# Last stage of a post-norm attention and mixture-of-experts layer: rows multiplied in ahead into eight PSUM banks, gate diagonals made during the experts, scaling on ScalarE, one load a batch

## What is computed

```
x = layernorm(x + attention(x))            # 16 heads of 8, causal
w = the two largest of softmax(x @ gate.T) # 14 experts, renormalised to sum 1
moe = w0 * expert[i0](x) + w1 * expert[i1](x)   # 128 -> 256, gelu, 256 -> 128
out = layernorm(x + clip(x + moe, -100, 100))
```

## Time and profile before

| | |
|---|---|
| median of 3 runs | 584.14 us (582.62 to 586.64) |
| the profiled execution's own time | 584.61 us |
| its span in the profile | 582.8 us |
| TensorE, VectorE, ScalarE, GpSimd busy | 454.8, 395.4, 319.7, 281.5 us |
| mean granted TensorE clock | 0.916 of full |
| experts, first to last TensorE work | 403.3 to 535.6 us |
| last stage, first load to last store issued | 540.6 to 577.8 us |

### The profile page before, as it was taken

The page is one execution under the profiler, slowest core; times in us unless marked ns, Lnnn a source line. Parts: engine busy times, 40 slices in busy tenths (PEclk is TensorE's granted clock), DMA queues, the critical chain, the costliest instruction groups (busy, mean ns, idle before and its releaser), DMA issues.

```text
span 582.8 us, 12473 instructions
## 1 busy us (share of the span) xinstructions
PE 454.8 (78%) x3544; PEld 279.2 (48%) x3576; DVE 395.4 (68%) x974; ACT 319.7 (55%) x771; POOL 281.5 (48%) x443
## 2 busy tenths in 40 slices
PE   4488999999999889999999997302877777766690
PEld 1244444444454444454454452102876666666690
DVE  4387679989889779889989984630454444444195
ACT  3065666776766756776767658102545454444570
POOL 2012233346556436556456448563565665556084
PEclk9599999999999989999999999755889898889697
DMA  7855942342542532442532301034322322210652
GB/s 130 254 164 168 299 147 87 112 152 86 156 147 75 156 120 81 151 148 74 156 120 89 90 30 43 10 98 95 96 79 69 83 76 69 69 58 20 180 164 91
DMA packets 82505, 65.46 MB, mean 112 GB/s; under 512 B 9207, under 2 KB 77950, under 8 KB 82449
## 3 DMA queue, kind: packets, MB, share of 16 engines
q1 hardware_dynamic: 75632, 55.52, 33.9%
q0 software_dynamic: 4512, 8.54, 4.4%
q10 hardware_dynamic: 2304, 0.74, 0.6%
HBM read 37.41 MB, written 25.85 MB: 109 GB/s over the span
## 4 chain that ended last, share of the span: by engine, by line
PE 58%; DVE 13%; issue 9%; ACT 5%; DMA 5%; POOL 3%; SPq 2%; another core or an unknown queue 2%; ACTq 0%; DVEq 0%; POOLq 0%
PE psum L873 10%; PE psum L855 9%; PE psum L832 8%; PE psum L1038 7%; PE psum L1027 7%; DVE nmax L1115 6%; PE psum L840 3%; PE psum L1017 3%; PE psum L892 3%; PE psum L928 2%; ACT probs L693 2%; PE psum L899 2%; POOL xs_dram L645 2%; DVE ov L1121 1%
## 5 line engine op out<-in xcount | busy, mean ns | idle before, releaser
L693 ACT ACTIVATE probs<-psum 128x512 f32<-128x512 f32 x320 | 182.3, 595 | 105.3 <-PE psum L855 73.5
L1115 DVE TENSOR_REDUCE nmax<-psum 128x2 f32<-128x1024 f32 (+3 forms) x224 | 198.0, 913 | 42.4 <-PE psum L840 42.3
L582 POOL TENSOR_SCALAR_AFFINE_SELECT probs<-probs 128x256 f32<-128x256 f32 (+1 forms) x192 | 88.1, 484 | 157.3 <-ACT probs L693 154.0
L832 PE MATMUL psum<-kst,qst 128*128 128x384 bf16 (+3 forms) x512 | 113.3, 306 | 14.1 <-DMA qst<-dq 10.1
L855 PE MATMUL psum<-qst,kst 128*128 128x384 bf16 (+3 forms) x481 | 102.5, 297 | 10.1 <-ACT probs L693 5.9
L654 POOL DMA_INDIRECT o_dram<-probs,xs x77 | 76.8, 998 | 63.0 <-DVE probs L1329 39.5
L873 PE MATMUL psum<-probs,vst 128*32 128x512 f32 (+3 forms) x1024 | 88.4, 441 | 1.2 <-DVE ov L1121 1.2
L840 PE MATMUL psum<-bmask,bident 128*128 128x256 bf16 (+1 forms) x320 | 81.8, 255 | 0.0
L855 PEld LDWEIGHTS psum<-qst,kst 128*128 128x128 bf16 x512 | 39.4, 98 | 75.7 <-ACT probs L693 34.9
L1038 PE MATMUL psum<-w_cur,hT_sb 128*128 128x128 f32 x308 | 56.2, 311 | 21.5 <-issue 11.5
L1329 DVE TENSOR_TENSOR probs<-psum,w_cur 128x128 f32<-128x128 f32 x77 | 22.3, 290 | 74.6 <-PE psum L1038 52.1
(11 more groups left out here) (165 smaller groups left out, 535.3 us busy)
## 6 DMA issues: line engine op xcount, KB each, us to landing
kst<-dk SPq DMA_DIRECT2D x64, 128.0 KB, 2.8
qst<-dq SPq DMA_DIRECT2D x32, 256.0 KB, 3.1
xs<-xs_dram SPq DMA_DIRECT2D x77, 66.0 KB
probs<-o_dram SPq DMA_DIRECT2D x16, 256.0 KB, 3.7
dk<-k SPq DMA_DIRECT2D x8, 384.0 KB, 2.9
dq<-q SPq DMA_DIRECT2D x8, 384.0 KB, 2.6
xT_sb<-in_xT SPq DMA_DIRECT2D x8, 256.0 KB
dk<-k SPq DMA_DIRECT2D x8, 256.0 KB, 2.5
```

The costliest lines, as they stand in the source:

```text
L582: pool.affine_select(out=view, in_=view, compare_op=ALU.is_ge, fill=0.0, base=0, pattern=[[0, view.shape[1]], [1, P]], channel_multiplier= ...
L693: act.activation(probs[:, c % 2, p, kk * T:(kk + 1) * T], ps_t[:, k % 2, :], ACT.Exp, scale=SCALE).then_inc(S["exp_done"], 1)
L832: pe.matmul(bank[:, at:at + w], qst[:, c, e, P * i:P * i + P], kst[:, c, h, e, 0:w], start=(at == 0), stop=False, skip_group_check=True)
L1115: last = dve.tensor_reduce(o, i, AX.X, ALU.max, negate=True)
```

## The change

- `slot` becomes batch * 1024 + p * 8 + i * 2 + k, so the eight results of a partition of a batch lie side by side in `o_dram`. A batch is loaded with one DMA of 512 KB in runs of 4 KB. The loads go into the space of `kst`, free since the attention.
- The gate operations on VectorE move ahead of its experts' loop. The 64 diagonals are made by ScalarE one by one, after steps 8 to 71 of its experts' code, into 64 buffers of their own.
- TensorE multiplies the rows of all eight batches by the identity right after its last expert tile, into eight PSUM banks; banks 4 to 7 wait for VectorE's last copy. With a load there, only the two diagonal products a block are left.
- VectorE no longer scales. The clipped sum goes to a buffer in `qst`; the addition of the rows is done in place in `xr`, by GpSimd for even batches and by VectorE for odd ones. VectorE does clip q, statistics of q-1, then the addition of q if q is odd.
- GpSimd makes the negated mean and, after the power, its product with the root: four operations a batch where there were two.
- ScalarE scales, in place in `xr`, four operations a batch with a scale and a bias column, and SyncE stores from `xr`, after it has issued all eight loads.
- The loops of the last stage are written out, and most turn-taking semaphore steps in it are gone.

```diff
-            pool.iota(slot[:], [[NTOK, TOPK], [P, NQ]], base=0, channel_multiplier=1,
+            pool.iota(slot[:], [[1, TOPK], [TOPK, NQ]], base=0, channel_multiplier=TOPK * NQ,
...
 # SyncE
+            def load_results(q):
+                u = q % FIN
+                if q >= FIN:
+                    sp.wait_ge(S["summed"], q - FIN + 1)
+                sp.dma_start(fin_o[:, u, :, :, :].rearrange("p i k d -> p (i k d)"),
+                             o_dram[q * T * TOPK:(q + 1) * T * TOPK, :].rearrange("(p r) d -> p (r d)", p=P)
+                             ).then_inc(o_loaded[u], 16)
+            for q in range(B):
+                load_results(q)
+            for q in range(B):
+                store_results(q)
...
 # GpSimd
+            for q in range(B + 1):
+                if q < B and q % 2 == 0:
+                    pool.wait_ge(S["clipped"], q + 1)
+                    rows = xr[:, q * T:(q + 1) * T]
+                    pool.tensor_tensor(rows, rows, fin[:, q % FIN, :], ALU.add).then_inc(S["residual_pool"], 1)
+                g = q - 1
+                if g >= 0:
+                    pool.wait_ge(S["fin_aggr"], NQ * (g + 1))
+                    if g >= 2:
+                        pool.wait_ge(S["fin_ready"], g - 1)
+                    rs, off = fin_rs[:, g % 2, :], fin_off[:, g % 2, :]
+                    pool.tensor_scalar(rs, fin_mv[:, g % 2, :, 1], EPS, None, ALU.add).then_inc(S["fin_vpe"], 1)
+                    pool.tensor_scalar(off, fin_mv[:, g % 2, :, 0], -1.0, None, ALU.mult).then_inc(S["fin_neg"], 1)
+                    pool.wait_ge(S["fin_vpe"], g + 1)
                     pool.tensor_tensor(rs, rs, mhalf[:], ALU.pow).then_inc(S["fin_rstd"], 1)
+                    pool.wait_ge(S["fin_rstd"], g + 1)
+                    pool.wait_ge(S["fin_neg"], g + 1)
+                    pool.tensor_tensor(off, off, rs, ALU.mult).then_inc(S["fin_off"], 1)
...
 # ScalarE
+            def diagonal(n):
+                q, k, i = n // (TOPK * NQ), n // NQ % TOPK, n % NQ
+                act.activation(diag[:, q, k, i, :], ident[:], ACT.Copy,
+                               scale=gw[:, 4 + k, q * NQ + i:q * NQ + i + 1]).then_inc(S["diag_ready"], 1)
             for j in range(NT + 1):
                 step(j)
+                if j == DIAG_FROM:
+                    act.wait_ge(S["gate_link"], 8)
+                if DIAG_FROM <= j < DIAG_FROM + B * TOPK * NQ:
+                    diagonal(j - DIAG_FROM)
+            for q in range(B):
+                act.wait_ge(S["fin_off"], q + 1)
+                for n in range(NQ):
+                    rows = xr[:, q * T + P * n:q * T + P * n + P]
+                    last = act.activation(rows, rows, ACT.Identity, bias=fin_off[:, q % 2, n:n + 1],
+                                          scale=fin_rs[:, q % 2, n:n + 1])
+                last.then_inc(S["fin_ready"], 1)
...
 # TensorE
+            pe.wait_ge(S["xsT_copied"], NT)
+            pe.wait_ge(S["gelu_done"], NT)
+            for q in range(B):
+                if q == 4:
+                    pe.wait_ge(S["y_copied"], NT)
                 for n in range(NQ):
+                    pe.matmul(psum[:, q, P * n:P * n + P], ident[:], xr[:, q * T + P * n:q * T + P * n + P],
+                              start=(n == 0), stop=False, skip_group_check=True)
+            pe.wait_ge(S["diag_ready"], B * TOPK * NQ)
+            for q in range(B):
+                pe.wait_ge(o_loaded[q % FIN], 16 * (q // FIN + 1))
+                for n in range(NQ):
                     for k in range(TOPK):
+                        last = pe.matmul(psum[:, q, P * n:P * n + P], diag[:, q, k, n, :], fin_o[:, q % FIN, n, k, :],
+                                         start=False, stop=(k == TOPK - 1), skip_group_check=True)
                 last.then_inc(S["summed"], 1)
...
 # VectorE
+            for q in range(B + 1):
+                if q < B:
+                    rows = xr[:, q * T:(q + 1) * T]
                     dve.wait_ge(S["summed"], q + 1)
+                    dve.tensor_scalar(fin[:, q % FIN, :], psum[:, q, :], 100.0, -100.0, ALU.min, ALU.max).then_inc(S["clipped"], 1)
+                g = q - 1
+                if g >= 0:
+                    if g % 2 == 0:
+                        dve.wait_ge(S["residual_pool"], g // 2 + 1)
+                    else:
+                        dve.wait_ge(S["residual_dve"], g // 2 + 1)
+                    if g >= 2:
+                        dve.wait_ge(S["fin_aggr"], NQ * (g - 1))
                     for n in range(NQ):
+                        dve.bn_stats(fin_st[:, g % 2, n, :], xr[:, g * T + P * n:g * T + P * n + P]).then_inc(S["fin_stats"], 1)
+                    if g >= 2:
+                        dve.wait_ge(S["fin_off"], g - 1)
                     for n in range(NQ):
+                        dve.wait_ge(S["fin_stats"], NQ * g + n + 1)
+                        dve.bn_aggr(fin_mv[:, g % 2, n, :], fin_st[:, g % 2, n, :]).then_inc(S["fin_aggr"], 1)
+                if q < B and q % 2:
+                    dve.wait_ge(S["clipped"], q + 1)
+                    dve.tensor_tensor(rows, rows, fin[:, q % FIN, :], ALU.add).then_inc(S["residual_dve"], 1)
```

More of the change, by code:

```diff
@@ L486, in _, with store_results @@
                 sp.wait_ge(y_scattered[n], 16 * -(-(NT - n) // STEP))
[L488 to L508, removed]
+            def load_results(q):
[5 more added lines that the diff above has]
+                             ).then_inc(o_loaded[u], 16)
+            def store_results(q):
+                sp.wait_ge(S["fin_ready"], q + 1)
+                sp.dma_start(out[q].rearrange("(i p) d -> p i d", p=P),
+                             xr[:, q * T:(q + 1) * T].rearrange("p (i d) -> p i d", i=NQ)).then_inc(out_stored[q % FIN], 16)
+            for q in range(B):
+                load_results(q)
+            for q in range(B):
+                store_results(q)
             for u in range(FIN):
@@ L794, in step @@
                     last.then_inc(S["gelu_done"], 1)
+            def diagonal(n):
+                q, k, i = n // (TOPK * NQ), n // NQ % TOPK, n % NQ
+                act.activation(diag[:, q, k, i, :], ident[:], ACT.Copy,
+                               scale=gw[:, 4 + k, q * NQ + i:q * NQ + i + 1]).then_inc(S["diag_ready"], 1)
             for j in range(NT + 1):
                 step(j)
-            def fin_step(i, r, _):
-                q, u, _ = lagged(i, r, 0, FIN)
-                if not (isinstance(q, int) and q < 2):
-                    act.wait_ge(S["summed"], q - 1)
-                for k in range(TOPK):
-                    for n in range(NQ):
-                        last = act.activation(diag[:, u % 2, k, n, :], ident[:], ACT.Copy,
-                                              scale=gw[:, 4 + k, bass.ds(q * NQ + n, 1)])
-                last.then_inc(S["diag_ready"], 1)
-            act.wait_ge(S["gate_link"], 8)
-            pipeline(act, fin_step, B, FIN, 0)
+                if j == DIAG_FROM:
[9 more added lines that the diff above has]
+                last.then_inc(S["fin_ready"], 1)
         @block.tensor
@@ L1370, in fin_step @@
                     for n in range(NQ):
-                        dve.bn_stats(fin_st[:, u % 2, n, :], fin[:, u, 2, P * n:P * n + P]).then_inc(S["fin_stats"], 1)
-                    if not (isinstance(q, int) and q < 2):
-                        dve.wait_ge(S["fin_ready"], q - 1)
-                        dve.sem_inc(S["dve_turn"], 1)
+                        dve.bn_stats(fin_st[:, g % 2, n, :], xr[:, g * T + P * n:g * T + P * n + P]).then_inc(S["fin_stats"], 1)
+                    if g >= 2:
+                        dve.wait_ge(S["fin_off"], g - 1)
@@ L1375, in fin_step @@
                     for n in range(NQ):
-                        dve.wait_ge(S["fin_stats"], NQ * q + n + 1)
-                        dve.sem_inc(S["dve_turn"], 1)
-                        dve.bn_aggr(fin_mv[:, u % 2, n, :], fin_st[:, u % 2, n, :]).then_inc(S["fin_aggr"], 1)
-                q, u, _ = lagged(i, r, 2, FIN)
-                if tile_live(q, B):
-                    dve.wait_ge(S["fin_rstd"], q + 1)
-                    for n in range(NQ):
-                        rows = fin[:, u, 2, P * n:P * n + P]
-                        last = dve.tensor_scalar(rows, rows, fin_mv[:, u % 2, n, 0:1], fin_rs[:, u % 2, n:n + 1],
-                                                 ALU.subtract, ALU.mult)
-                    last.then_inc(S["fin_ready"], 1)
```

62 lines of the change are left out of this document (14 added, 48 removed).

## The result

The changed kernel takes 578.1 us in the median of 4 runs (577.45 to 579.36), the kernel before 583.4 us beside it (582.52 to 586.64). The ratio is 0.9885, 95% interval 0.9848 to 0.9921: 5.3 us faster, where 3.5 us were forecast. The profiled execution of the changed kernel took 577.45 us, with a span of 575.4.

What follows compares the result with a forecast made beforehand. It took the last stage to wait for the last scatter, first load and TensorE's slow-clocked batch 0, then VectorE's 2.90 us a batch. Gains of 4.1 + 0.7 - 1.3 = 3.5 us from 584.61 led to 580.8 us, range 576.0 to 586.5.

Steps and rivals of the forecast that it cites:

- First load: Last stage's start: one 512 KB transfer for batch 0 instead of two of 256 KB, data there at 544.1 us.
- the term of 4.1 us: Start of the last stage: first clip at 546.1 instead of 550.19, with TensorE's clock full for batch 0.
- Rows ahead: Before the load: 32 identity products on TensorE, 7.0 us from 535.6 on, hidden by the 8.5 us up to the load.
- The cycle afterwards: Last stage after the first clip: GpSimd becomes the bound, 2.90 us a batch falls to 2.68; stage 26.5 instead of 27.2.
- The rival of a faster cycle: Last stage: GpSimd's chains shorter, VectorE's 4.05 us for two batches counts; up to 4 us less, 576.8; chance 0.18.
- The port: Last stage: VectorE's odd additions delay GpSimd at the shared port; 1.0 us taken, bounds 0 to 2.6.
- Gate operations ahead of the experts: Before VectorE's first weight copy: at most 2.9 us, hidden while TensorE stands idle; cost 0.
- Diagonals: Experts: 64 on ScalarE at 0.305 us each; 1.3 us taken as cost, bounds -1 and 19.5.
- The rival of ScalarE's pace: Experts: ScalarE's work delays the next tile's copy; at 0.22 us a diagonal, 14 us, 593.5 in total; chance 0.12.
- Scatter order: Expert rows scattered to other places in `o_dram`: 0, bounds -0.3 and +1 us at the last landing.
- The sign that failed: Experts: stretch of 132 to 135 us expected; wrong if it grows by more than 3 us or shrinks.
- Sum: Whole kernel: start 4.1, cycle 0.7, experts -1.3, 3.5 us gained; 581.1 for the profiled execution, 580.8 given as median.

Runs made afterwards that it cites:

- cold late rows: Changed kernel with the identity products put back behind the load, in each batch's turn; ratio to the kernel before 0.9999 (0.9969 to 1.0029).
- the first pair: The changed kernel and the kernel before, measured beside each other and first profiled: 578.1 against 583.4 us, ratio 0.9885.
- the other chip: Changed kernel unedited, run again on a chip where the kernel before takes 555.7 us: 550.3 us, ratio 0.9903.
- the version that does it: Changed kernel with rows of batches 4 to 7 held for the last scatter but one, most additions on VectorE, last scaling shared: 578.1 us, ratio 0.9878.

## Why the prediction was right, point by point

580.8 us were forecast, with a range from 576.0 to 586.5, and 578.1 were measured. The mechanism was right: work ahead keeps the clock up, the rest of batch 0 is short, and GpSimd becomes the bound behind it. The sizes of the parts were not, and that the total came out this near is in part luck.

- **First load.** The first clip was forecast for 546.1 and came at 546.04, by luck: the load was issued 0.6 us earlier than before (539.96), for reasons outside the sum. Counted from the issue, 5.5 us were forecast and 6.1 measured: 0.3 more for the load to come in and 0.2 more for batch 0 (2.1 us from its first product to the clip, not 1.9). The clock stayed up, as forecast, and the run with cold late rows shows that it would have fallen. So the term of 4.1 us was too high: 3.6 against the first profile, in which the clock rose late, and 2.7 against the second profile of the kernel before.
- **Rows ahead.** 7.0 us forecast, 7.3 measured, hidden. Their second effect was not in the sum: with them behind the load TensorE needs 2.68 us a batch and the stage takes 1.9 us more. It was hidden before, when 2.90 was the pace, and counts now.
- **The cycle afterwards.** GpSimd became the bound, as said, and the run with all additions on it confirms it. The term was mis-sized: 0.7 us of gain were forecast for the stage and 2.8 measured. A chain takes 1.91 us, not 2.03 (the power took 1.04, not 1.11), and two batches 5.04, not 5.35: 1.2 us over the eight batches. Lead-in 3.6 as forecast, last scaling 1.65. The rival of a faster cycle was right in that the chains are shorter, and wrong in that VectorE would set the pace: it waits for GpSimd.
- **The port.** 1.0 us taken, 0.34 measured. By the Trainium skill's rule ("SBUF — State Buffer", section "SBUF: two separate sides") each holder blocks the other for its whole operation. The runs agree for a short GpSimd operation that starts early in VectorE's addition (0.57 instead of 0.23, ending just behind it), and disagree where the addition starts during the power: both keep their length (1.04 and 0.66, in the changed kernel at 553.57 and 554.09). Three of the changed kernel's four additions fall into a power.
- **Gate operations ahead of the experts.** The first tile came 1.6 us later in the first profile; over all profiles of kernels with them early it came at 402.5 to 405.5, and at 403.3 and 405.0 with them late. No cost can be seen, as forecast.
- **Diagonals.** 1.3 us taken, nothing seen. The rival of ScalarE's pace, 14 us, is refuted for 64 diagonals, even on the chip whose TensorE runs without stops. ScalarE is busy there for 79.1 of the 93.6 us, and 64 more came with 3.7 us.
- **Scatter order.** 0 forecast, and nothing seen at the last landing (2.08 us against 2.11).
- **The sign that failed.** The prediction called itself wrong if the experts' stretch shrank, and in the first pair it did, by 1.1 us. That sign was of no use: with the same code the stretch took 127.9 to 133.5 us from profile to profile. The last scaling ended 24.4 us after the first clip, also outside the 26 to 27 that were to show it.
- **Sum.** 3.5 us forecast: 4.1 + 0.7 - 1.3. (581.1 less the 0.5 is 580.6, not 580.8; nothing hangs on it.) The medians give 5.3. From the load's issue to the end of the span the two profiles of the kernel before take 42.2 and 41.3 us and the changed kernel 35.4, so 5.9 to 6.8 us are gained there, where 4.8 were forecast. The start was too high by 0.5 to 1.4. The stage came out 2.1 below the 26.5 forecast for it, 1.9 of it from the two mis-sized terms above (1.2 and 0.7). The end of the span came 4.9 to 5.2 us behind the last scaling in every variant in which ScalarE alone scales, and 5.4 and 5.5 before: 0.2 to 0.6 us gained, and I have no cause for it. What lies ahead of the load's issue varies by more than it differs: in the first pair the experts gave 1.1 us, the last scatters 1.1, and the start took 1.6.

## What to carry to other kernels

If TensorE waits for a transfer, give it work that is needed anyway until the transfer lands: it pays once by the clock and once by what is no longer behind the load. On the other chip it didn't last: TensorE ended the experts 15.5 us before the load was issued, and the clock had fallen again. So it seems better to place such work by the event that releases the load than by the engine's own last tile; no run here shows that, since the version that does it never ran on that chip. When one engine's work is taken away, add up the next engine with its own durations, down to operations of 0.2 us: eight chains of four such operations are the bound of this stage.

## What the runs showed of the hardware that was not expected

- The same code of the experts takes TensorE 128 to 134 us in all profiles but those of one chip, and 94 to 95 us there. In the first profile of the changed kernel 18 weight loads of one line wait 19.8 us for nothing that the profile shows, up to 2.0 us each; on the other chip there is none. The whole kernel before takes 582 to 585 us and 555.7 us. That these are waits for instructions is a guess.
- A GpSimd operation of 0.23 us that starts early in a VectorE addition with two SBUF inputs ends 0.09 us behind it. A power of 1.04 us and an addition of 0.66 us that starts in its midst don't disturb each other.
- Loads of 512 KB in runs of 4 KB flow at 389 to 397 GB/s (in stretches of 2 us) and pairs of 256 KB in runs of 512 bytes at 284 to 288, but the first clip, with four batches in flight, comes at most 0.3 us earlier for it.
